# Circular correlation attention and LoRA linear layer: softmax weights masked in PSUM and turned by DMA transposes instead of TensorE transposes

## The reference

```python
x = x + autocorrelation(layernorm(x), ctx, ctx)
x = x + ffn(layernorm(x))          # x @ W + bias + LoRA terms

# autocorrelation, for every batch and every one of the 2048 channels
corr = ifft(fft(q) * conj(fft(k))).real          # over the 512 positions
w, idx = top_k(corr, 12); w = softmax(w)
out[pos] = sum_i w[i] * v[min(idx[i] + pos, L - 1)]
```

## Time and profile before

| | us |
|---|---|
| median of 3 runs | 3106.81 |
| range of the runs | 3106.17 to 3109.11 |
| time of the profiled execution | 3107.9 |
| its span in the profile | 3106.1 |
| TensorE busy in that span | 3018.6 |
| VectorE busy | 2077.8 |
| GpSimd busy | 1659.4 |
| ScalarE busy | 1120.5 |

### The profile page before, as it was taken

The page is one execution under the profiler, slowest core; times in us unless marked ns, Lnnn a source line. Parts: engine busy times, 40 slices in busy tenths (PEclk is TensorE's granted clock), DMA queues, the critical chain, the costliest instruction groups (busy, mean ns, idle before and its releaser), DMA issues. The chain is left out here.

```text
span 3106.1 us, 37964 instructions
## 1 busy us (share of the span) xinstructions
PE 3018.6 (97%) x14387; PEld 1647.6 (53%) x14387; DVE 2077.8 (67%) x2742; ACT 1120.5 (36%) x1696; POOL 1659.4 (53%) x753
## 2 busy tenths in 40 slices
PE   5999999999999999999977999999999999999999
PEld 3566565665656566665643444444444444444444
DVE  6889898989989999999994445444444443344322
ACT  4666666666656666555521011110111111011100
POOL 4898898988979898988842122221221122112210
PEclk9999999999999999999998999999999999999999
DMA  6334434344444534334159444345344534434321
GB/s 229 134 125 150 153 135 170 119 156 146 136 162 146 173 135 165 126 129 160 64 191 267 155 132 125 117 136 150 105 130 125 145 105 134 153 109 136 95 79 41
DMA packets 281220, 430.27 MB, mean 139 GB/s; under 512 B 147489, under 2 KB 164001, under 8 KB 265633
## 3 DMA queue, kind: packets, MB, share of 16 engines
q1 hardware_dynamic: 145888, 394.43, 36.7%
q10 hardware_dynamic: 135168, 33.57, 6.0%
HBM read 308.15 MB, written 86.25 MB: 127 GB/s over the span
## 5 line engine op out<-in xcount | busy, mean ns | idle before, releaser
L1439 PE MATMUL ps<-w_hi,h_hi 128*128 128x512 f16 x2048 | 776.5, 379 | 1.8 <-PEq L308 1.8
L1440 PE MATMUL ps<-w_lo,h_hi 128*128 128x512 f16 x2048 | 776.4, 379 | 0.0
L1441 PE MATMUL ps<-w_hi,h_lo 128*128 128x512 f16 x2048 | 776.4, 379 | 0.0
L1313 POOL TENSOR_TENSOR xt<-xt,vl 128x2048 f32<-128x2048 f32 x31 | 139.8, 4509 | 890.2 <-DMA xt<-x_scratch 653.9
L887 PE MATMUL ps<-op,it 128*128 128x512 f32 x1024 | 447.4, 595 | 12.8 <-DVE op L1034 12.8
L805 PE MATMUL ps<-wt,fp 128*128 128x512 f16 x1536 | 338.8, 380 | 2.1 <-DVE wt L1001 1.4
L1441 PEld LDWEIGHTS ps<-w_hi,h_lo 128*128 128x128 f16 x2048 | 200.5, 98 | 241.8 <-issue 0.3
L1439 PEld LDWEIGHTS ps<-w_hi,h_hi 128*128 128x128 f16 x2048 | 200.8, 98 | 238.9 <-issue 3.2
L887 PEld LDWEIGHTS ps<-op,it 128*128 128x128 f32 x1024 | 195.1, 191 | 247.4 <-issue 230.9
L1440 PEld LDWEIGHTS ps<-w_lo,h_hi 128*128 128x128 f16 x2048 | 200.5, 98 | 234.9 <-issue 0.6
L805 PEld LDWEIGHTS ps<-wt,fp 128*128 128x128 f16 x1536 | 150.5, 98 | 184.7 <-issue 2.2
(11 more groups left out here) (191 smaller groups left out, 5724.8 us busy)
## 6 DMA issues: line engine op xcount, KB each, us to landing
sg<-lora_ab SPq DMA_DIRECT2D x112, 512.0 KB, 4.8
xv<-x SPq DMA_DIRECT2D x33, 1024.0 KB, 5.2
cg<-ctx SPq DMA_DIRECT2D x32, 1024.0 KB, 5.2
x_scratch<-xv SPq DMA_DIRECT2D x32, 1024.0 KB, 4.2
xt<-x_scratch SPq DMA_DIRECT2D x32, 1024.0 KB, 5.1
out<-xt SPq DMA_DIRECT2D x31, 1024.0 KB, 4.0
xg<-x SPq DMA_DIRECT2D x30, 1024.0 KB, 8.0
xrow<-x SPq DMA_DIRECT2D x24, 1024.0 KB, 5.0
```

Source lines behind the costliest of these rows:

```text
L1313: nc.gpsimd.tensor_tensor(xt[:, k, :], xt[:, k, :], vl[:, :], ALU.add).then_inc(vl_ok, 1)
L1439: nc.tensor.matmul(ps[:, c, :], h_hi[k][:, i, :], w_hi[c][:, i, :], start=(i == 0), stop=False)
L1440: nc.tensor.matmul(ps[:, c, :], h_hi[k][:, i, :], w_lo[c][:, i, :], start=False, stop=False)
L1441: last = nc.tensor.matmul(ps[:, c, :], h_lo[k][:, i, :], w_hi[c][:, i, :], start=False, stop=(i == KT - 1))
```

## The change

The masks write in place in PSUM (banks 0 to 3) and not to `wd`. ACT takes the fp16 high part from there before anything is turned (`high_of_w` in place of `transposed_out`), DVE the rest, both in channel x lag layout in `w16`, two views of the tile `mi`. SP then issues four DMA transposes per group (`turn_weights`): high and rest, each in two halves of 128 x 1024, into `wt`, which is laid out by channel block. PE's sixteen transposes are gone; its `forward_w` reads `wt` with four runs of 128 columns per matmul. DVE's order changes: `w_rest` of the next group comes right behind the masks instead of at the head of the next step, the additions of output banks 4 and 5 are done ahead of the masks, and those of 6 and 7 after `w_rest`. SP's loop over batches 1 to 3 is written out instead of being a hardware loop.

```diff
-            wt = sb("wt", [P, 2, 4, GC], FP16, st)
+            wt = sb("wt", [P, 2, CT, 4, P], FP16, st)
+            w16 = [mi[:, 2 * k:2 * k + 2, :].rearrange("p a c -> p (a c)").bitcast(FP16).rearrange("p (j c) -> p j c", c=L) for k in range(2)]
...
+                    def turn_weights(b, g):
+                        n = GPB * b + g
+                        if later(b, g):
+                            sp.wait_ge(w_spec, 8 * n)
+                        for a, split in enumerate((wt_hi, wt_lo)):
+                            for k in range(2):
+                                sp.wait_ge(split, 4 * n + 2 * k + 2)
+                                sp.dma_start_transpose(wt[:, a, 2 * k:2 * k + 2, :, :].rearrange("p j l c -> p (j l) c"),
+                                                       w16[a][:, 2 * k:2 * k + 2, :].rearrange("p j l -> p (j l)")).then_inc(s_wt[a][k], 16)
...
                             store_weights(b, g, 1)
+                        if lead:
+                            turn_weights(*ahead(b, g, 1))
+                        if convert:
                             if lead:
                                 sp.wait_ge(s_wst, 32 * piece(b, g, 1) + 32)
...
                     load_context(0, 3)
+                    turn_weights(0, 0)
                     sp.wait_ge(var_ok, 2)
...
-                    with sp.Fori(1, B // 2) as b:
+                    for b in range(1, B // 2):
...
-                    def transposed_out(b, g):
+                    def high_of_w(b, g):
                         n = GPB * b + g
-                        if later(b, g):
-                            act.wait_ge(w_spec, 8 * n)
-                        for k in range(4):
-                            act.wait_ge(wt_spec, 4 * n + k + 1)
-                            nc.scalar.activation(wt[:, 0, k, :], ps[:, k, :], ACT.Copy, scale=WSCALE).then_inc(wt_hi, 1)
+                        for j in range(CT):
+                            act.wait_ge(w_ready, 4 * n + j + 1)
+                            nc.scalar.activation(w16[0][:, j, :], ps[:, j, :], ACT.Copy, scale=WSCALE).then_inc(wt_hi, 1)
...
+                    def forward_w(bank, kind, part):
+                        dst = ps[:, bank, :].rearrange("p (j c) -> p j c", c=P)
+                        for k in range(2):
+                            for i, (tab, val) in enumerate(((0, 0), (1, 0), (0, 1))):
+                                last = nc.tensor.matmul(dst, fp[:, tab, k, kind, :], wt[:, val, :, 2 * part + k, :],
...
                         pe.wait_ge(wt_lo, 4 * n + 4)
+                        for a in range(2):
+                            for k in range(2):
+                                pe.wait_ge(s_wt[a][k], 16 * n + 16)
...
                     def step(b, g, more, lead, scale=False):
-                        transpose_w(b, g)
...
                         nc.vector.reciprocal(rz[:, :], zsum[:, :]).then_inc(rz_ok, 1)
+                        if output:
+                            add_output(*output, (0, 1))
                         for j in range(CT):
...
-                            nc.vector.scalar_tensor_tensor(out=wd[:, j, :], in0=eo[:, j, :], scalar=NEG, in1=ps[:, j, :],
+                            nc.vector.scalar_tensor_tensor(out=ps[:, j, :], in0=eo[:, j, :], scalar=NEG, in1=ps[:, j, :],
                                                            op0=ALU.is_le, op1=ALU.mult).then_inc(w_ready, 1)
...
                         if lead:
-                            top_lags(*ahead(b, g, 1), (b, g) if convert else None)
+                            top_lags(*ahead(b, g, 1), (b, g) if convert else None, (b, g))
+                            w_rest(*ahead(b, g, 1))
...
-                        add_output(b, g)
+                        add_output(b, g, (2, 3) if lead else range(4))
```

More of the change, by code:

```diff
@@ L286, in build @@
             w_ready = sem("w_ready", st)
-            wt_spec = sem("wt_spec", st)
+            s_wt = [[sem(f"s_wt{a}{k}", st) for k in range(2)] for a in range(2)]
             wt_hi = sem("wt_hi", st)
@@ L703, in step @@
                     def step(b, g, more, lead, far, rows, convert, first=False):
-                        transposed_out(b, g)
+                        high_of_w(b, g)
                         if first:
@@ L832, in q_spectrum @@
                             forward_pair(4 + i, i, (qh, ql[k]), i // 2).then_inc(q_spec, 1)
[L834 to L840, removed]
+                    def forward_w(bank, kind, part):
[3 more added lines that the diff above has]
+                                last = nc.tensor.matmul(dst, fp[:, tab, k, kind, :], wt[:, val, :, 2 * part + k, :],
+                                                        start=(k == 0 and i == 0), stop=(k == 1 and i == 2))
+                        return last
                     def top_to_row():
@@ L859, in weight_spectra @@
                                 pe.wait_ge(top_read, 1)
-                            forward_pair(i, (ER, EI)[i % 2], (wt[:, 0], wt[:, 1]), i // 2).then_inc(w_spec, 1)
+                            forward_w(i, (ER, EI)[i % 2], i // 2).then_inc(w_spec, 1)
                         if lead:
                             pe.wait_ge(cprod, 4 * n + 8)
+                        else:
+                            pe.wait_ge(out_add, 4 * n)
                         for i in range(4):
-                            forward_pair(4 + i, (OR, OI)[i % 2], (wt[:, 0], wt[:, 1]), i // 2).then_inc(w_spec, 1)
+                            forward_w(4 + i, (OR, OI)[i % 2], i // 2).then_inc(w_spec, 1)
                     def correlation(b, g):
@@ L996, in w_rest @@
                         n = GPB * b + g
[L997 to L1001, removed]
+                        for j in range(CT):
+                            dve.wait_ge(wt_hi, 4 * n + j + 1)
+                            nc.vector.scalar_tensor_tensor(out=w16[1][:, j, :], in0=ps[:, j, :], scalar=WSCALE, in1=w16[0][:, j, :],
                                                            op0=ALU.mult, op1=ALU.subtract).then_inc(wt_lo, 1)
@@ L1034, in products_odd, with top_lags @@
                         nc.vector.tensor_tensor(op[:, 1, OI, :], ps[:, 7, :], cr[:, 1, :], ALU.subtract).then_inc(hi_sum, 1)
-                    def top_lags(b, g, convert):
+                    def top_lags(b, g, convert, output):
                         m = GPB * b + g
@@ L1062, in top_lags @@
                         if later(b, g):
-                            dve.wait_ge(wt_spec, 4 * m)
                             dve.wait_ge(op_sum, 6 * m - 1)
                         nc.vector.reciprocal(rz[:, :], zsum[:, :]).then_inc(rz_ok, 1)
+                        if output:
+                            add_output(*output, (0, 1))
                         for j in range(CT):
@@ L1068, in top_lags, with add_output @@
                             dve.wait_ge(w_scaled, 4 * m + j + 1)
-                            nc.vector.scalar_tensor_tensor(out=wd[:, j, :], in0=eo[:, j, :], scalar=NEG, in1=ps[:, j, :],
+                            nc.vector.scalar_tensor_tensor(out=ps[:, j, :], in0=eo[:, j, :], scalar=NEG, in1=ps[:, j, :],
                                                            op0=ALU.is_le, op1=ALU.mult).then_inc(w_ready, 1)
-                    def add_output(b, g):
+                    def add_output(b, g, banks):
                         n = GPB * b + g
@@ L1075, in add_output @@
                         for i, t in enumerate(TURN):
+                            if i not in banks:
+                                continue
                             dve.wait_ge(out_spec, 4 * n + i + 1)
@@ L1102, in step @@
                     def step(b, g, lead, convert, first=False):
-                        w_rest(b, g)
                         if first or not convert and later(b, g):
@@ L1140, in _ @@
                     first_statistics(1)
-                    top_lags(0, 0, None)
+                    top_lags(0, 0, None, None)
+                    w_rest(0, 0)
                     for g in range(GPB):
```

## The result

The change makes the kernel slower: a median of 3134.66 us over 4 runs (3129.17 to 3140.05) against 3106.69, a ratio of 1.0086 with a 95% interval of 1.0075 to 1.0098. Timed again as a control it gave 3136.57 us, a ratio of 1.0095 (1.0078 to 1.0112). The profiled execution took 3129.17 us, its span is 3127.4; it is the fastest of the four, so the profile shows 21.3 us of the 28 us by which the medians differ. The forecast was 3085, faster, with a range from 3053 to 3130.

What follows compares the result with a forecast made beforehand. PE was taken to set most steps, with DVE's chain almost as long and setting seven later ones. Gains of 11.6 + 14.0 + 1.4 less 4 and 1 gave 22 us, hence 3085 us, range 3053 to 3130.

Steps and rivals of the forecast that it cites:

- Before batch 4: Fifteen steps: PE waits 1.0 us for the transposes, 0.77 of 1.75 us remains, step 48.05, gain 11.6 us.
- 1 MB load: Load ahead in SP's queue before batch 4, said to keep engines busy until 766.4, so the four transposes finish at 772.2.
- M: End of a group's last mask; SP was to issue transposes from about M - 0.4, the last landing at M + 6.55.
- Batches 5 and 6: Eight later steps set by PE: nothing is waited for, so 8 x 1.75 = 14.0 us gained.
- b: Part of a step from DVE's first product to last mask; read as 34.4 us in batches 5 and 6, 37.3 in 4 and 7.
- a: Part from start of weight spectra to DVE's first product; taken as 5.2 us plus 0.1 in batches 4 and 7.
- c: Part from last mask to next weight spectra; the last transpose was to land 6.55 us after the mask when alone.
- What is queued behind the four: Loads and stores behind the transposes on SP come 2 to 4 us later; late pieces of W cost 4 us.
- Rival A: Everything hidden: PE sets all 31 steps, 3054 us, or 3068 with the slow steps kept; chance 0.18.
- Batches 4 and 7: Seven later steps set by the DVE chain: 49.6 against 49.8 us, 1.4 us gained in all.
- Start and end: First group gains 2 us, the end loses 3: -1 together, with ends -6 and +2.
- C: Rival: slower, PE waiting for transposes ahead of the weight spectra; 3178 us at 6.2 us landing, 3128 for 1.4; chance 0.28.

Runs made afterwards that it cites:

- f4: e2 with DVE's rest of the second W piece taken before the second search, its store and the next load ahead of the transposes; 3087.55 us.
- e4: The changed kernel with the four transposes issued ahead of the 1 MB xrow load before batch 4; 3217.12 us.
- f2: The kernel before with only the output sums moved around the masks, TensorE transposes kept; 3106.45 us.
- e2: The changed kernel plus one wait on POOL, so that DVE's two sums over eo start before POOL's odd-half sum; 3109.67 us.
- f1: The kernel before with the same single wait on POOL as in e2; 3101.88 us.
- g1: The changed kernel with the early rest of W of f4 but without the wait on POOL; 3107.57 us.

## Why the prediction was wrong

*What held.* PE bounds most steps before; f4's later steps show that removing the transposes gives up to 1.75 us where PE bounds (47.17 against 48.82). Before batch 4 the step was forecast at 48.05 and measured at 48.17, a gain of 9.9 us where 11.6 were forecast. The strided read and the masks into PSUM cost nothing that can be seen: 10.52 us for 48 matmuls, 2.47 to 2.54 us for four masks. Landing took 3.3 us where I took 3.2. The granted clock is 1.00 in all steps from group 1 to 30, but for the one from group 16, which has 0.94 before and after.

*Right by a wrong reason.* The 7.6 us from mask to weight spectra before batch 4 came out of the 1 MB load that I took to hold the transposes up. e4 moved the load away, and the part stayed at 7.6. What takes the time is issue: the first starts at 759.35, 0.2 us behind the last mask at 759.12, since ACT writes the highs only after all four of its divisions, and four issues take 5.37 us, 1.34 each. I had M - 0.4 and 1.25. The fourth lands 3.2 us behind its own start, as soon as the first does, so the three ahead of it do not hold its transfer up. The 0.6 us that I added for the semaphore stood in no row: PE starts 0.14 us behind the last landing. In the later batches, without the load, I therefore had 6.55 and it is 7.3 to 7.5. The Trainium skill ("DMA: Bandwidth & Descriptors", Latency and other measured facts) has the faster transfer that I weighed there, 261 GB/s or more, an estimated 1.0 us for each instead of 1.46. By these runs it would have shortened no more than the landing of the last one, by at most 0.5 us as an estimate, and not the 1.8 us that I took: with the same landing times the issue sets the pace.

*The step that failed* is "Batches 5 and 6", 8 x 1.75 = 14.0 us of gain. Measured: 8 x (50.76 - 48.82) = 15.5 us of loss, 29.5 off, 3.7 a step. By parts, mean of the eight steps: b is 37.0 instead of 34.9 (2.1 us), a is 6.3 instead of 5.3 (1.0), c is 7.4 instead of 6.8 (0.6).

The term that was mis-sized most is b. I had seen that DVE needs 34.4 us in one step and 37.3 in another, called it another kind of step, and carried each number over as if it belonged to the batch. Most of the difference belongs to a race, and the earlier trace rows show its two outcomes. The step of the earlier trace rows was also a bad sample: DVE's rest of W took 2.23 us in it and 3.1 in the seven others, whose b is 35.3. So of the 2.1 us, 0.6 were in my reading (with the moved sums the eight have 35.5 in f2, where the race is still won) and about 1.6 are the lost race. Rival A spoke of the alignment of DVE and POOL, but only as a way to gain. e2, f1, f4 and g1 show the race by its removal and its return. That PE's query spectrum, no longer held behind the transposes, is what brings POOL early is my reading of the timelines. POOL's first sum of the even half, in the step of the lines above, before and after:

```profile
1377.97 2.37 POOL L485 TENSOR_TENSOR mr<-mr 128x1024 f32<-128x1024 f32 x1
```

```profile
1386.11 2.35 POOL L500 TENSOR_TENSOR mr<-mr 128x1024 f32<-128x1024 f32 x1 [3.42 <-DVE mr L1028]
```

Before, POOL came to it straight from the sums of the query spectrum and was the later one; now these are done early, it waits 3.4 us for DVE's product, and from there on it is right behind DVE. In g1, where the product is in time, it still waits 1.2 us and the race is lost. f2 excludes only the order of the output sums. No run delayed the query spectrum by itself, none moved `w_rest` alone, and none kept SP's hardware loop.

The term for a was in the text with a wrong place and size. "What is queued behind the four" put the late piece of W in three or four steps of batch 5, as a delay of ACT's spectra copies, at -4 us. It holds the products up in eleven of the fourteen steps from group 17 on, and it delays DVE's rest of W, which stands ahead of the products: on the chain that had just become the longest. I had costed the queue by who waits for the load, but had not asked what stands behind that waiter on DVE.

*Batches 4 and 7.* The forecast had seven equal steps of 49.80 us and a gain of 1.4 us. Before the change only three of them take 49.86; two take 48.8, the one from group 16 takes 56.9 and the last 46.1. Measured is a loss of 10.4 us over the seven. Part a makes up 8.0 of it, 2.9 in the step from group 16 alone, where it grew from 10.8 to 13.7.

*Start and end.* Forecast was a gain of 2 for the first group and a loss of 3 at the end. The first weight spectra start 2.3 us later, and they take 12.31 us instead of 10.52: they stand behind PE's wait of 13.7 us, and the granted clock of that step is 0.96 where it was 1.00. At the last group, PE waited 12.12 us instead of 6.66, and c was 7.27 there instead of 5.14, against +1.8 forecast:

```profile
1629.95 12.41 PE L852 MATMUL ps<-wt,fp 128*128 128x512 f16 x48 [12.12 <-DMA wt<-mi]
```

*The rivals.* The time is one of C, just above the 3130 at which I had cut it in two, but the mechanism is not: the landing times stayed at 3.3, at most 4.0. Its arithmetic was right in size: the miss of 50 us is 1.6 us for each of 31 steps, and C had 3128 for 1.4.

## What to carry to other kernels

When an engine is relieved of work, look at the second longest chain as carefully as at the first: two kinds of the same step in one trace are a warning that its length depends on which of two engines comes first, and the change may pick the other one. A transfer put into an ordered queue costs its issue time to everything behind it; walk that queue down to the engine that waits, and then to what that engine does next. A small wait that fixes the order of two colliding instructions can be worth more than the edit it accompanies.

## What the runs showed of the hardware

The engines do not meet only at semaphores, as was said at the start: DVE and POOL slow each other when both add tiles in SBUF, and where the two start close together the first instruction of the one that starts first is spared: DVE's two sums took 1.23 and 2.32 us when it led by 0.1 us, 1.97 and 3.41 when POOL led; POOL's sum of 128 x 512 took 1.29 us when it led and 2.30 when it did not. A DMA transpose of 128 x 1024 fp16 occupied the issuing queue for 1.33 us, one of 128 x 2048 for 2.17, and they landed after 3.3 and 4.6 us (medians). Four of the first kind, one behind the other, were set by issue: 5.37 us, with the fourth landing 3.2 us behind its own start like the first. Beside a load of 512 KB from another queue the same transposes landed after 4.4 us in the median, and the issue of the second took 2.5 us instead of 1.3.
